# Attention of four experts on Trainium2: one written-out pipeline over 256 heads, with the row maxima split on GpSimd

## The chip, the cores and the metric

One core of a Trainium2 chip runs the whole kernel in one launch. The metric is the device time of an execution in microseconds (us), the median of repeated runs. TensorE (PE) multiplies, VectorE (DVE) and ScalarE (ACT) work on its results, GpSimd (POOL) does small work between SBUF buffers, and SyncE's queue (SPq) issues the DMAs.

## The reference, cut to what matters

The kernel computes a small language-model tower. The change touches one part of it, the attention inside each of 4 experts, for 4 batches of 512 tokens (16 blocks), with 16 heads of 16 channels, followed by the input products of a two-way LSTM:

```python
q, k, v = (heads(q), heads(k), heads(v))
attn = softmax(einsum('bhqd,bhkd->bhqk', q, k) * SCALE)
o = einsum('bhqk,bhkd->bhqd', attn, v).transpose(0, 2, 1, 3).reshape(h.shape)
h = o @ aow + aob
zg = xt @ Wi + h @ Wh + b      # x @ Wi + b is made here for all steps and both ways; the recurrence adds h @ Wh
```

## The kernel before, in words

The stages run one after another: embedding, causal attention, router, `experts_encode`, `experts_attend`, `recurrence`, `experts_after`, a state-space layer and a mixer. `experts_attend` is what changes, with three lines of `recurrence` that read its result.

**A head.** q and k arrive as bfloat16 parts, 96 rows per head (`load_heads`, L864, twelve DMAs for half of a block's heads). `score` (L975, matmul L981) makes one of four 128x512 tiles of scores in bank 0 or 1, by turns; `largest` (L1049, L1051) takes the negated row maximum on VectorE and frees the bank. `split` (L1054 to L1068) makes three bfloat16 parts of the four maxima with four tiny, dependent VectorE instructions. `turn_maxima` (L984, L990) turns the parts into rows 96 to 98 of q with four small matmuls, and `keep_rows` (L1088, ScalarE) stores them. `score_t` (L994, L1003) makes a transposed tile of scores with the maximum already taken off, in banks 2 to 4, and `exponent` (L1091, L1096, ScalarE) makes the exponentials. `values` (L1006, L1014) multiplies four heads' exponentials by v side by side in bank 6, and `keep_values` (L1100) copies the result of four heads out.

**A block.** After its 16 heads a block's result is turned (`turn_values`, L909), divided by the softmax sums (`divide`, L917 and L919, VectorE), turned back (`turn_divided`, L927; `keep_divided`, L935), projected (`project`, L943; `keep_projected`, L950) and multiplied by the LSTM's input weights: 16 products of 128x512 with two matmuls each (`product`, L874, L883). `keep_product` (L888, L894, VectorE) adds a bias and writes into `zs`; `store_products` (L897) sends 2 MB per way to DRAM.

**Order.** `attend(e, b, products)` is one block of instructions on all engines, of 18 written-out steps. In step h stand the scores of head h, the turned maxima of head h-1 and the transposed scores of head h-2. The first block of an expert has `products=False`. The other three run in a loop and also carry the turning, projection and products of the block before: the turning at their start, one product in each step from 2 on. All these products use bank 7 alone (`BESIDE`), one matmul of a product between `score_t` 2 and `score` 2, the other behind `values`:

```python
if products and h >= 2:
    product(pe, h - 2, 0, BESIDE)     # before score(h, 2)
...
if products and h >= 2:
    product(pe, h - 2, 1, BESIDE)     # last of the step
```

A product's first matmul waits for `z_kept` of the product before (L883). On VectorE a step is `keep_product`, two `largest`, two `largest`, `split`. The products of an expert's last block stand in a block of their own, with nothing beside them and two banks (`ALONE`). At every boundary all engines meet and semaphores are cleared. `zs` is `[P, 2, S, BLOCKS]`, so a product's 512 values lie 32 bytes apart.

Of the kernel before, what the change touches and what calls it, by code (L numbers as in the profile page):

```python
# [820 lines left out]
RING = 8  # L821


def experts_attend(core, d):


# [11 lines left out]
    with ExitStack() as ctx:  # L838
# [4 lines left out]
        vx = core.sb(ctx, "bvx", [P, BT, NH, DH + 1])  # L843
# [11 lines left out]
        zs = core.sb(ctx, "bzs", [P, 2, S, BLOCKS])  # L855
        (loaded, filled, scored, maxed, part1, part2, part3, rested, rows_mm, rows_kept, scored_t, exped, valued, o_kept,
         o_turned, inverted, on_done, on_turned, oT_kept, a_mm, a_kept, z_mm, z_kept) = core.sems(
            "ba", "loaded filled scored maxed part1 part2 part3 rested rowsmm rowskept scoredt exped valued okept "
                  "oturned inverted on onturned oTkept amm akept zmm zkept")
        qk_in = core.sems("ba", "qkin0 qkin1")  # L860
        (vx_in,) = core.sems("ba", "vxin")
        z_stored = core.sems("ba", "zstored0 zstored1")

        def load_heads(sp, slab, half):  # L864
            heads = slice(half * NH // 2, (half + 1) * NH // 2)
            for side, dst in ((0, qp), (1, kp)):
                for n, pair in enumerate(PAIRS):
                    src = d["qk"][slab, side, pair[side]].rearrange("(h r) n -> r h n", r=DH)
                    sp.dma_start(dst[n * DH:(n + 1) * DH, heads], src[:, heads]).then_inc(qk_in[half], 16)

        BESIDE, ALONE = (7,), (7, 5)
        HEADS_IN = 2 * len(PAIRS) * 16

        def product(pe, n, k, banks):  # L874

            way, block = divmod(n, BLOCKS)
            if k == 0:
                if n == 0:
                    pe.wait_ge(a_kept, KH)
                elif n >= len(banks):  # L880
                    pe.wait_ge(z_kept, n - len(banks) + 1)
            at = ATT["wi"] + (way * KH + k) * G4 + block * P
            last = nc.tensor.matmul(bank[banks[n % len(banks)]][:], w[:, at:at + P], aT[:, k], start=k == 0,  # L883
                                    stop=k == KH - 1)
            if k == KH - 1:
                last.then_inc(z_mm, 1)

        def keep_product(dve, n, banks, e, b):  # L888

            way, block = divmod(n, BLOCKS)  # L890
            dve.wait_ge(z_mm, n + 1)
            if block == 0:
                dve.wait_ge(z_stored[way], 16 * (e * B + b) + 1)
            nc.vector.tensor_scalar(zs[:, way, :, block], bank[banks[n % len(banks)]][:],  # L894
                                    cols[:, COLS["lb"] + n:COLS["lb"] + n + 1], None, ALU.add).then_inc(z_kept, 1)

        def store_products(sp, way, e, b):  # L897

            sp.wait_ge(z_kept, BLOCKS * (way + 1))
            sp.dma_start(d["zx"][way, e, b], zs[:, way].rearrange("p t n -> p (t n)")).then_inc(z_stored[way], 16)  # L900

        turn_banks = [bank[2], bank[3], bank[4], bank[7]]
        project_banks = [bank[7], bank[4]]

        def turn_values(pe):

            for qt in range(BT):
                for g in range(4):
                    last = nc.tensor.transpose(turn_banks[qt][:, g * P:(g + 1) * P], o[:, g, qt * P:(qt + 1) * P],  # L909
                                               core.ident[:])  # L910
                last.then_inc(o_turned, 1)

        def divide(dve):
            for qt in range(BT):
                heads = turn_banks[qt][:].rearrange("p (h r) -> p h r", r=32)
                dve.wait_ge(o_turned, qt + 1)
                nc.vector.reciprocal(inv[:, qt], heads[:, :, DH]).then_inc(inverted, 1)  # L917
                dve.wait_ge(inverted, qt + 1)
                nc.vector.tensor_tensor(on[:, qt], heads[:, :, 0:DH],  # L919
                                        inv[:, qt].unsqueeze(2).broadcast_to([P, NH, DH]), ALU.mult).then_inc(on_done, 1)  # L920

        def turn_divided(pe):

            for qt in range(BT):
                pe.wait_ge(on_done, max(qt + 1, 2))
                for k in range(KH):
                    last = nc.tensor.transpose(turn_banks[k][:, qt * P:(qt + 1) * P],  # L927
                                               on[:, qt, k * NH // KH:(k + 1) * NH // KH].rearrange("p h r -> p (h r)"),
                                               core.ident[:])
            last.then_inc(on_turned, 1)  # L930

        def keep_divided(act):
            act.wait_ge(on_turned, 1)
            for k in range(KH):
                nc.scalar.activation(oT[:, k], turn_banks[k][:], ACT.Copy).then_inc(oT_kept, 1)  # L935

        def project(pe):

            pe.wait_ge(oT_kept, KH)
            for m in range(KH):  # L940
                for k in range(KH):
                    at = ATT["aow"] + k * DM + m * P
                    last = nc.tensor.matmul(project_banks[m][:], w[:, at:at + P], oT[:, k], start=k == 0,  # L943
                                            stop=k == KH - 1)
                last.then_inc(a_mm, 1)

        def keep_projected(act):
            for m in range(KH):
                act.wait_ge(a_mm, m + 1)
                nc.scalar.activation(aT[:, m], project_banks[m][:], ACT.Identity,  # L950
                                     bias=cols[:, COLS["aob"] + m:COLS["aob"] + m + 1]).then_inc(a_kept, 1)

        def attend(e, b, products):


            with nc.Block() as block:
                @block.sync
                def _(sp):
                    if not products:
                        sp.dma_start(w[:], d["w_attend"][e]).then_inc(loaded, 16)  # L960
                        sp.dma_start(cols[:], d["cols"][e]).then_inc(loaded, 16)
                    load_heads(sp, e * B + b, 1)
                    sp.dma_start(vx[:].rearrange("p t h r -> p (t h r)"), d["vx"][e * B + b]).then_inc(vx_in, 16)
                    sp.wait_ge(scored_t, BT * NH // 2)
                    load_heads(sp, e * B + b + 1, 0)
                    if products:
                        for way in range(2):
                            store_products(sp, way, e, b - 1)
                    sp.wait_ge(qk_in[0], HEADS_IN)
                    if not products:  # L970
                        sp.wait_ge(loaded, 32)

                @block.tensor
                def _(pe):
                    def score(h, qt):  # L975

                        if h == NH // 2 and qt == 0:
                            pe.wait_ge(qk_in[1], HEADS_IN)
                        if BT * h + qt >= 2:
                            pe.wait_ge(maxed, BT * h + qt - 1)  # L980
                        nc.tensor.matmul(bank[qt % 2][:], qp[0:KROWS, h, qt * P:(qt + 1) * P], kp[0:KROWS, h],  # L981
                                         start=True, stop=True).then_inc(scored, 1)

                    def turn_maxima(h):  # L984

                        pe.wait_ge(part3, h + 1)
                        if h > 0:
                            pe.wait_ge(rows_kept, h)
                        for qt in range(BT):
                            last = nc.tensor.matmul(bank[5][KROWS:KROWS + 3, qt * P:(qt + 1) * P],  # L990
                                                    maxparts[:, h % 2, qt], ident16[:], start=True, stop=True)
                        last.then_inc(rows_mm, 1)

                    def score_t(h, kt):  # L994

                        n = BT * h + kt
                        if kt == 0:
                            pe.wait_ge(rows_kept, h + 1)
                        if products and n == 2:
                            pe.wait_ge(a_kept, KH)  # L1000
                        if n >= 3:
                            pe.wait_ge(exped, n - 2)
                        nc.tensor.matmul(bank[2 + n % 3][:], kp[:, h, kt * P:(kt + 1) * P], qp[:, h], start=True,  # L1003
                                         stop=True).then_inc(scored_t, 1)

# [171 lines left out]
        with nc.Fori(0, E - 1) as e:  # L1177
            expert(e, False)
# [826 lines left out]
```

## Time and profile before

| | us |
|---|---|
| median of 3 runs | 5915.8 (5911.99 to 5916.03) |
| the profiled execution | 5917.21, its span 5915.4 |
| `experts_attend` within the span | 779 to 2475 |
| `recurrence` | about 2475 to 5353 |
| mean granted TensorE clock | 0.963 of full speed |

The profile lists for each engine what it did and what it waited for. An instruction is named by line, engine and operation, then output<-input. A product or any other float32 matmul leaves two MATMUL records. "xN" in the timeline merges N instructions: the time beside it is from the first's start to the last's end.

### The profile page before, as it was taken

The page shows a single profiled execution, that of the slowest core. Times are in us where ns is not written, and L with a number is a line of the kernel's source. Part 1 is how long each engine was busy: PE and PEld are TensorE (multiplying, and loading weights), DVE is VectorE, ACT ScalarE, POOL GpSimd, SP SyncE. Part 2 cuts the span into 40 slices and gives each one's busy share as a digit, 9 for nine tenths or more (in the row PEclk, how much of TensorE's full clock was granted, in tenths as well). Part 3 has the DMA queues.
Part 4 walks back from the last instruction along what each step waited for, and adds up shares of the span by engine and source line. Part 5 has one row for each costly group of instructions (what it writes and reads, how often), then busy time and mean ns, then how long its engine had stood idle before and what let it go on. Part 6 is the DMA issues. An engine that isn't in the chain of part 4 may idle for free. (4 is left out here: it accounts for less than half of the span.)

```text
span 5915.4 us, 261478 instructions
## 1 busy us (share of the span) xinstructions
PE 5379.3 (91%) x108704; PEld 3590.6 (61%) x108704; DVE 4411.6 (75%) x20301; ACT 2334.2 (39%) x8423; POOL 944.5 (16%) x4109
## 2 busy tenths in 40 slices
PE   7878879989889998699999999999999999998895
PEld 4545523323323333288888888888888888884442
DVE  4546567666676676699999999999999999993224
ACT  2334444444354354433333333333333333333332
POOL 0000000000000000033333333333333333330000
PEclk9989989989989999899999999999999999999997
DMA  0003353334343334401111011111011111002110
GB/s 12 0 20 119 112 105 79 73 82 86 86 78 84 93 58 82 153 15 36 26 31 36 20 30 36 28 29 36 21 29 36 23 34 36 16 19 79 58 43 11
DMA packets 378664, 302.83 MB, mean 51 GB/s; under 512 B 146074, under 2 KB 358682, under 8 KB 373563
## 3 DMA queue, kind: packets, MB, share of 16 engines
q1 hardware_dynamic: 378510, 301.15, 21.4%
q8 instruction: 52, 0.85, 0.1%
q14 instruction: 102, 0.83, 0.0%
HBM read 182.09 MB, written 120.59 MB: 51 GB/s over the span
## 5 line engine op out<-in xcount | busy, mean ns | idle before, releaser
L1318 PE MATMUL bank<-lparts,lstate 128*32 128x256 bf16 x98304 | 2784.8, 273 | 103.2 <-DVE lstate L1364 55.5
L1318 PEld LDWEIGHTS bank<-lparts,lstate 128*32 128x32 bf16 x98304 | 2459.1, 97 | 429.4 <-DVE lstate L1364 252.4
L1395 ACT ACTIVATE ltc<-lgc 128x16 f32<-128x16 f32 x2049 | 442.6, 216 | 1763.8 <-DVE lgc L1350 1763.5
L1329 DVE STREAM_TRANSPOSE ltz<-bank 128x256 f32<-128x256 f32 x2048 | 920.8, 450 | 98.3 <-PE bank L1318 19.9
L1051 DVE TENSOR_REDUCE bnegmax<-bank 128x1 f32<-128x512 f32 x1024 | 650.1, 679 | 257.0 <-PE bank L981 255.7
L1411 POOL TENSOR_TENSOR wh<-lgate,ltc 128x16 f32<-128x16 f32 x2052 | 465.6, 227 | 1936.7 <-ACT ltc L1395 1862.5
L1096 ACT ACTIVATE wh<-bank 128x512 f32<-128x512 f32 x1024 | 554.9, 598 | 296.9 <-PE bank L1003 290.0
L1418 POOL COPY ltz<-wh 128x64 f32<-128x64 f32 x2048 | 605.8, 296 | 0.0
L883 PE MATMUL bank<-xT,bw 128*128 128x512 f32 x1024 | 537.0, 626 | 56.6 <-DVE bzs L894 50.2
L1336 DVE TENSOR_TENSOR lhalf<-ltz 128x128 f32<-128x128 f32 x2048 | 576.8, 282 | 12.1 <-POOL ltz L1418 11.4
L1346 DVE TENSOR_TENSOR lprod<-lgate,lgc 128x32 f32<-128x32 f32 x2049 | 472.7, 231 | 46.2 <-ACT lgc L1391 46.2
L1390 ACT ACTIVATE lgate<-lz 128x48 f32<-128x48 f32 x2048 | 499.8, 244 | 0.4
L894 DVE TENSOR_SCALAR bzs<-bank,bcols 128x512 f32<-128x512 f32 x256 | 292.3, 1142 | 251.9 <-PE bank L883 251.4
L981 PE MATMUL bank<-bkp,bqp 96*128 96x512 bf16 x1024 | 346.8, 410 | 121.5 <-DVE bnegmax L1051 37.6
L1340 DVE TENSOR_TENSOR lz<-lhalf 128x64 f32<-128x64 f32 x2048 | 438.6, 214 | 0.0
L1391 ACT ACTIVATE lgc<-lz 128x16 f32<-128x16 f32 x2048 | 408.2, 199 | 0.0
L1285 POOL MEMSET lstate<- 128x512 f32 x1 | 0.5, 525 | 2474.6 <-POOLq L61 2474.6
L981 PEld LDWEIGHTS bank<-bkp,bqp 96*128 96x128 bf16 x1024 | 98.0, 100 | 454.4 <-DVE bnegmax L1051 264.9
L883 PEld LDWEIGHTS bank<-xT,bw 128*128 128x128 f32 x1024 | 168.0, 189 | 332.4 <-DVE bzs L894 162.5
L1354 DVE TENSOR_TENSOR lstate<-lgate,ltc 128x16 f32<-128x16 f32 x2050 | 366.9, 179 | 3.3 <-ACT ltc L1395 0.3
L1359 DVE TENSOR_TENSOR lstate<-lstate 128x16 f32<-128x16 f32 x2048 | 347.8, 170 | 0.0
L1364 DVE TENSOR_TENSOR lstate<-lstate 128x16 f32<-128x16 f32 x2048 | 338.5, 165 | 0.0
(211 smaller groups left out, 4848.0 us busy)
## 6 DMA issues: line engine op xcount, KB each, us to landing
zx<-bzs SPq DMA_DIRECT2D x32, 2048.0 KB, 6.8
wh<-zx SPq DMA_DIRECT2D x64, 1024.0 KB, 7.4
bqp<-qk SPq DMA_DIRECT2D x198, 128.0 KB, 4.7
bkp<-qk SPq DMA_DIRECT2D x198, 128.0 KB, 7.9
qk<-eparts SPq DMA_DIRECT2D x96, 256.0 KB, 2.6
hs<-wh SPq DMA_DIRECT2D x32, 512.0 KB, 5.8
cmemT<-hs SPq DMA_DIRECT2D x32, 512.0 KB, 4.3
bw<-in_w_attend SPq DMA_DIRECT2D x4, 2304.0 KB, 11.5
```

The source lines that it names most:

```text
L883: last = nc.tensor.matmul(bank[banks[n % len(banks)]][:], w[:, at:at + P], aT[:, k], start=k == 0, stop=k == KH - 1)
L981: nc.tensor.matmul(bank[qt % 2][:], qp[0:KROWS, h, qt * P:(qt + 1) * P], kp[0:KROWS, h], start=True, stop=True).then_inc(scored, 1)
L1051: nc.vector.tensor_reduce(negmax[:, h, qt:qt + 1], bank[qt % 2][:], AX.X, ALU.max, negate=True).then_inc(maxed, 1)
L1096: nc.scalar.activation(pT[:, h % RING, kt], bank[2 + n % 3][:], ACT.Exp).then_inc(exped, 1)
L1318: last = nc.tensor.matmul(bank[x][32 * q:32 * q + 32, 0:256], top[:, x, e, k].rearrange("p m r -> p (m r)"), parts[:, way, g, k, n, e, q], ...
L1329: nc.vector.transpose(tz[:, x].rearrange("p (n w) -> p n w", w=SLOT)[:, :, 0:32], bank[x][:, 0:256].rearrange("p (n c) -> p n c", n=BLOCKS ...
L1336: nc.vector.tensor_tensor(half[:, x], rows[:, 1:3], rows[:, 3:5], ALU.add).then_inc(paired[x], 1)
L1346: nc.vector.tensor_tensor(prod[:, x], gate[:, x, 0:2], gc[:, x], ALU.mult).then_inc(multiplied[x], 1)
L1390: nc.scalar.activation(gate[:, x], z[:, x, 0:3], ACT.Sigmoid)
L1395: nc.scalar.activation(tc[:, x], gc[:, x, 1], ACT.Tanh).then_inc(tanhed[x], 1)
L1411: return nc.gpsimd.tensor_tensor(out.rearrange("p k (e b) -> p k e b", e=2), units(gate[:, x, 2]), units(tc[:, x]), ALU.mult)
L1418: nc.gpsimd.tensor_copy(rows, zx[:, way, i // ZX_STEPS % 2, 8 * g:8 * g + 8, at].rearrange("p r n -> p n r")).then_inc(placed[x], 1)
```

## The change

Both kinds of block, the loops over blocks and experts and the lone products go. One block of instructions is written out for 256 heads (step j is head j) and ends with the last block's turning and products. The turning of a block now stands in steps 6 to 10 after its last head's step, its 16 products in the eleven steps behind those, as 1, 2, 1, 2, ... products a step, all through bank 7; both matmuls of a product stand together. `turn_maxima` moves behind the products. The tail alone uses banks 7, 5, 0 and 1. GpSimd does `split`. Weights are loaded in three pieces, each as its last use is over, and v has two buffers. `zs` becomes `[P, 2, S/16, BLOCKS, 16]`: 16 values of a product stand side by side, and `recurrence` reads that order. The copy of block 0's q and k behind the last block's in DRAM goes. The other helpers (`score_t`, `values`, `exponent` and so on) do the same work with running counts.

```diff
+ZX_STEPS = 16
...
-        vx = core.sb(ctx, "bvx", [P, BT, NH, DH + 1])
+        vx = core.sb(ctx, "bvx", [P, 2, BT, NH, DH + 1])
...
-        zs = core.sb(ctx, "bzs", [P, 2, S, BLOCKS])
...
+        zs = core.sb(ctx, "bzs", [P, 2, S // ZX_STEPS, BLOCKS, ZX_STEPS])
...
+        TURN_AT, PRODUCTS_AT = 6, 11
+        PRODUCTS_IN_STEP = (1, 2, 1, 2, 1, 2, 1, 2, 1, 2, 1)
+        LAST_STEP = HEADS + 6
+        LATE_BANKS = (7, 5, 0, 1)
+        def products_of(j):
+            at = (j - PRODUCTS_AT) % NH
+            slab = (j - PRODUCTS_AT) // NH - 1
+            if slab < 0 or at >= len(PRODUCTS_IN_STEP):
+                return slab, 0, 0
+            first = sum(PRODUCTS_IN_STEP[:at])
+            return slab, first, first + PRODUCTS_IN_STEP[at]
+        def turned_in(j):
+            slab = (j - TURN_AT) // NH - 1
+            return (slab, (j - TURN_AT) % NH) if 0 <= slab < SLABS - 1 else (slab, -1)
...
+        def product_bank(slab, n):
+            return bank[LATE_BANKS[n % len(LATE_BANKS)] if slab == SLABS - 1 else 7]
+        def turn_bank(slab, n):
+            return bank[(2, 3, 4, 7)[n] if slab == SLABS - 1 else 7]
...
+                    if 0 < slab < SLABS:
+                        sp.wait_ge(scored_t, BT * NH * slab)
+                        load_heads(slab, 1)
+                    if slab >= 2:
+                        store_products(slab - 2, 1)
+                        if (slab - 2) % B == B - 1 and slab < SLABS:
+                            sp.wait_ge(z_mm, NH * (slab - 1))
+                            load_in_weights((slab - 1) // B, 1)
+                            load_columns((slab - 1) // B)
+                    if slab < SLABS - 1:
+                        if slab > 0:
+                            sp.wait_ge(valued, NH * slab)
+                        load_values(slab + 1)
+                        sp.wait_ge(scored_t, BT * NH * slab + BT * NH // 2)
+                        load_heads(slab + 1, 0)
+                    if slab > 0:
+                        if slab == SLABS:
+                            sp.wait_ge(valued, NH * SLABS)
+                            sp.dma_start(core.wh[:], d["wh"]).then_inc(wh_in, 16)
+                        if slab % B == 0 and slab < SLABS:
+                            sp.wait_ge(a_mm, KH * slab)
+                            load_out_weights(slab // B)
+                        store_products(slab - 1, 0)
...
+                for j in range(LAST_STEP):
+                    slab, at = turned_in(j)
+                    made, first, end = products_of(j)
+                    if j < HEADS:
+                        score(j, 0)
+                        score(j, 1)
+                    if 2 <= j < HEADS + 2:
+                        for kt in range(3):
+                            score_t(j - 2, kt)
+                    if at == 1:
+                        turn_values(slab, 1)
+                    elif at == 2:
+                        turn_values(slab, 3)
+                    elif at == 3:
+                        turn_divided(slab, 0)
+                    elif at == 4:
+                        project(slab, 0)
+                    elif end > first:
+                        for k in range(KH):
+                            product(made, first, k)
+                    if j < HEADS:
+                        score(j, 2)
+                        score(j, 3)
+                    if 2 <= j < HEADS + 2:
+                        score_t(j - 2, 3)
+                    if at == 0:
+                        turn_values(slab, 0)
+                    elif at == 1:
+                        turn_values(slab, 2)
+                    elif at == 3:
+                        turn_divided(slab, 1)
+                    elif at == 4:
+                        project(slab, 1)
+                    elif end > first + 1:
+                        for k in range(KH):
+                            product(made, end - 1, k)
+                    if 1 <= j < HEADS + 1:
+                        turn_maxima(j - 1)
...
+                def keep_product(slab, n):
...
+                        dve.wait_ge(z_stored[way], 16 * slab)
+                    nc.vector.tensor_scalar(zs[:, way, :, block],
+                                            product_bank(slab, n)[:].rearrange("p (c t) -> p c t", t=ZX_STEPS),
+                                            cols[:, COLS["lb"] + n:COLS["lb"] + n + 1], None, ALU.add).then_inc(z_kept, 1)
...
+                for j in range(LAST_STEP + 1):
+                    slab, at = turned_in(j)
+                    earlier, first_before, end_before = products_of(j - 1)
+                    made, first, end = products_of(j)
+                    if end_before > first_before + 1:
+                        keep_product(earlier, end_before - 1)
+                    if at == 1:
+                        divide(slab, 0)
+                    elif at == 2:
+                        divide(slab, 2)
+                    if j < HEADS:
+                        largest(j, 0)
+                        largest(j, 1)
+                    if end > first:
+                        keep_product(made, first)
+                    if at == 1:
+                        divide(slab, 1)
+                    elif at == 2:
+                        divide(slab, 3)
+                    if j < HEADS:
+                        largest(j, 2)
+                        largest(j, 3)
...
+            @block.gpsimd
+            def _(pool):
+                def split(j):
+                    negated = negmax[:, j % NH]
+                    parts = [maxparts[:, j % 2, :, n] for n in range(3)]
+                    pool.wait_ge(maxed, BT * (j + 1))
+                    if j >= 2:
+                        pool.wait_ge(rows_mm, j - 1)
+                    nc.gpsimd.tensor_copy(parts[0], negated).then_inc(part1, 1)
+                    pool.wait_ge(part1, j + 1)
+                    if j > 0:
+                        pool.wait_ge(part3, j)
+                    nc.gpsimd.tensor_tensor(rest[:], negated, parts[0], ALU.subtract).then_inc(rested, 1)
+                    pool.wait_ge(rested, j + 1)
+                    nc.gpsimd.tensor_copy(parts[1], rest[:]).then_inc(part2, 1)
+                    pool.wait_ge(part2, j + 1)
+                    nc.gpsimd.tensor_tensor(parts[2], rest[:], parts[1], ALU.subtract).then_inc(part3, 1)
+                for j in range(HEADS):
+                    split(j)
...
+                def keep_divided(slab, k):
+                    act.wait_ge(on_turned, KH * slab + k + 1)
+                    if k == 0 and slab > 0:
+                        act.wait_ge(a_mm, KH * slab)
+                    nc.scalar.activation(oT[:, k], turn_bank(slab, k)[:], ACT.Copy).then_inc(oT_kept, 1)
...
-            "p (w f g t n) -> p w f g t n", w=2, f=2, g=E * B, t=ZX_STEPS)
+            "p (w f g n t) -> p w f g n t", w=2, f=2, g=E * B, t=ZX_STEPS)
...
-            sp.dma_start(zx[:, way, buf].rearrange("p g t n -> p g (t n)"),
+            sp.dma_start(zx[:, way, buf].rearrange("p g n t -> p g (n t)"),
...
-                    nc.gpsimd.tensor_copy(rows, zx[:, way, i // ZX_STEPS % 2, 8 * g:8 * g + 8, at].rearrange(
+                    nc.gpsimd.tensor_copy(rows, zx[:, way, i // ZX_STEPS % 2, 8 * g:8 * g + 8, :, at].rearrange(
```

ScalarE's step is `keep_values` (every fourth), `keep_divided(1)` or `keep_projected(1)` where due, three `exponent`, `keep_divided(0)` or `keep_projected(0)` where due, the fourth `exponent`, `keep_rows`.

## Rows read from the trace of the kernel before

**Rows 1.** The profile's page: the span, and the busy time of each engine.
```profile
span 5915.4 us, 261478 instructions
PE 5379.3 (91%) x108704; PEld 3590.6 (61%) x108704; DVE 4411.6 (75%) x20301; ACT 2334.2 (39%) x8423; POOL 944.5 (16%) x4109
```
**Rows 2.** Windows: window, length, busy us (x instructions) per engine, PEclk, DMA share, GB/s.
```profile
779.00:2475.00 1696.00, 1515.92 (x6656) 532.62 (x6656) 1123.67 (x2432) 786.70 (x1411) 0.00 (x0) 0.95 0.39 86
...
782.30:852.70 70.40, 62.68 (x322) 17.42 (x323) 50.42 (x128) 47.22 (x85) 0.00 (x0) 0.90 0.48 88
853.00:953.50 100.50, 91.39 (x415) 32.05 (x412) 69.58 (x152) 48.99 (x88) 0.00 (x0) 0.98 0.37 74
...
1154.67:1203.51 48.84, 36.15 (x96) 17.70 (x97) 21.02 (x24) 3.74 (x5) 0.00 (x0) 0.89 0.31 120
```
**Rows 3.** Timeline, one head with a product: start us, us, instruction, idle before and releaser.
```profile
895.20 1.26 DVE L1051 TENSOR_REDUCE bnegmax<-bank 128x1 f32<-128x512 f32 x2
...
895.41 1.13 PE L883 MATMUL bank<-xT,bw 128*128 128x512 f32 x2
...
896.38 0.60 PE L981 MATMUL bank<-bkp,bqp 96*128 96x512 bf16 x2
...
896.80 1.29 DVE L1051 TENSOR_REDUCE bnegmax<-bank 128x1 f32<-128x512 f32 x2 [0.34 <-PE bank L981]
...
896.90 0.38 PE L990 MATMUL bank<-bident,bmaxparts 128*3 128x128 bf16 x4
...
897.54 1.05 PE L1014 MATMUL bank<-wh,bvx 128*17 128x512 f32 x8
...
898.12 0.18 DVE L1060 CAST bmaxparts<-bnegmax 128x4 bf16<-128x4 f32 x1
...
898.52 1.13 PE L883 MATMUL bank<-xT,bw 128*128 128x512 f32 x2
...
899.49 0.60 PE L981 MATMUL bank<-bkp,bqp 96*128 96x512 bf16 x2
...
899.69 1.14 DVE L894 TENSOR_SCALAR bzs<-bank,bcols 128x512 f32<-128x512 f32 x1 [0.78 <-PE bank L883]
...
899.92 0.81 PE L1003 MATMUL bank<-bqp,bkp 99*128 99x512 bf16 x3
900.34 1.57 ACT L1096 ACTIVATE wh<-bank 128x512 f32<-128x512 f32 x3 [1.80 <-PE bank L1003]
...
900.89 1.12 PE L883 MATMUL bank<-xT,bw 128*128 128x512 f32 x2 [0.15 <-DVE bzs L894]
```
**Rows 4.** Timeline, one head of a block without products.
```profile
818.40 0.61 PE L981 MATMUL bank<-bkp,bqp 96*128 96x512 bf16 x2
...
822.12 0.61 PE L981 MATMUL bank<-bkp,bqp 96*128 96x512 bf16 x2
```
**Rows 5.** Timeline, the start of a block that turns and projects the block before.
```profile
953.57 1.03 PE L981 MATMUL bank<-bkp,bqp 96*128 96x512 bf16 x2 [2.41 <-PEq L61]
...
954.40 3.07 PE L909 MATMUL bank<-ident,bo 128*128 128x128 f32 x16
...
955.49 0.26 DVE L917 RECIPROCAL binv<-bank 128x16 f32<-128x16 f32 x1
955.79 0.42 DVE L919 TENSOR_TENSOR xn<-bank,binv 128x256 f32<-128x256 f32 x1
```
**Rows 6.** Lines, shapes kept apart: two VectorE operations; busy us, mean ns, idle before.
```profile
L894 DVE TENSOR_SCALAR bzs<-bank,bcols 128x512 f32<-128x512 f32 x256 | 292.3, 1142 | 251.9 <-PE bank L883 251.4
...
L740 DVE TENSOR_SCALAR eqk<-bank,ecols 128x512 f32<-128x512 f32 x32 | 24.0, 751 | 61.0 <-PE bank L660 61.0
```
**Rows 7.** Lines, shapes kept apart: a small GpSimd operation of the recurrence.
```profile
L1411 POOL TENSOR_TENSOR wh<-lgate,ltc 128x16 f32<-128x16 f32 x2052 | 465.6, 227 | 1936.7 <-ACT ltc L1395 1862.5 <-issue 37.3 <-POOLq L1261 36.8
```
**Rows 8.** Timeline, the end of the stage.
```profile
2437.67 27.73 PE L883 MATMUL bank<-xT,bw 128*128 128x512 f32 x64 [0.78 <-ACT xT L950]
...
2475.03 0.53 POOL L1285 MEMSET lstate<- 128x512 f32 x1 [2474.58 <-POOLq L61]
```

More of the change, by code:

```diff
@@ L862, in experts_attend @@
         z_stored = core.sems("ba", "zstored0 zstored1")
[L864 to L871, printed above, removed]
@@ L872, in experts_attend @@
-        HEADS_IN = 2 * len(PAIRS) * 16
[L874 to L951, printed above, removed]
@@ L1122, in experts_attend, with project_bank @@
+        def turned_in(j):
[5 more added lines that the diff above has]
+            return bank[(2, 3, 4, 7)[n] if slab == SLABS - 1 else 7]
+        def project_bank(slab, n):
+            return bank[(4, 7)[n] if slab == SLABS - 1 else 7]
         with nc.Block() as block:
@@ L1124, in _, with load_heads @@
             def _(sp):
-                sp.dma_start(d["qk"][E * B], d["qk"][0]).then_inc(filled, 16)
-                load_heads(sp, 0, 0)
-                sp.wait_ge(qk_in[0], HEADS_IN)
-                sp.wait_ge(filled, 16)
+                def load_heads(slab, half):
+                    heads = slice(half * NH // 2, (half + 1) * NH // 2)
+                    for side, dst in ((0, qp), (1, kp)):
+                        for n, pair in enumerate(PAIRS):
+                            src = d["qk"][slab, side, pair[side]].rearrange("(h r) n -> r h n", r=DH)
+                            sp.dma_start(dst[n * DH:(n + 1) * DH, heads], src[:, heads]).then_inc(qk_in[half], 16)
@@ new lines, in load_values, with load_out_weights, load_in_weights @@
+                def load_values(slab):
+                    sp.dma_start(vx[:, slab % 2].rearrange("p t h r -> p (t h r)"), d["vx"][slab]
+                                 ).then_inc(vx_in[slab % 2], 16)
+                def load_out_weights(e):
+                    sp.dma_start(w[:, 0:ATT["wi"]], d["w_attend"][e, :, 0:ATT["wi"]]).then_inc(out_w_in, 16)
+                def load_in_weights(e, way):
+                    lo, hi = (ATT["wi"] + (way + n) * KH * G4 for n in range(2))
+                    sp.dma_start(w[:, lo:hi], d["w_attend"][e, :, lo:hi]).then_inc(wi_in[way], 16)
@@ new lines, in _ @@
+                load_out_weights(0)
+                load_columns(0)
+                for way in range(2):
+                    load_in_weights(0, way)
+                for slab in range(SLABS + 1):
+                    if 0 < slab < SLABS:
[21 more added lines that the diff above has]
+                        store_products(slab - 1, 0)
+                        if slab % B == 0 and slab < SLABS:
+                            sp.wait_ge(z_mm, NH * (slab - 1) + BLOCKS)
+                            load_in_weights(slab // B, 0)
@@ L1177, in experts_attend, with largest, divide @@
-        with nc.Fori(0, E - 1) as e:
-            expert(e, False)
-        expert(E - 1, True)
+                def largest(j, qt):
+                    dve.wait_ge(scored, BT * j + qt + 1)
+                    if j >= NH and qt == 0:
+                        dve.wait_ge(part3, j - NH + 1)
+                    nc.vector.tensor_reduce(negmax[:, j % NH, qt:qt + 1], bank[qt % 2][:], AX.X, ALU.max,
+                                            negate=True).then_inc(maxed, 1)
+                def divide(slab, qt):
+                    heads = turn_bank(slab, qt)[:].rearrange("p (h r) -> p h r", r=32)
+                    dve.wait_ge(o_turned, BT * slab + qt + 1)
+                    if qt == 0 and slab > 0:
+                        dve.wait_ge(on_turned, KH * slab)
+                        dve.wait_ge(on_done, BT * slab)
+                    nc.vector.reciprocal(inv[:, qt], heads[:, :, DH]).then_inc(inverted, 1)
+                    dve.wait_ge(inverted, BT * slab + qt + 1)
+                    nc.vector.tensor_tensor(on[:, qt], heads[:, :, 0:DH],
+                                            inv[:, qt].unsqueeze(2).broadcast_to([P, NH, DH]), ALU.mult).then_inc(on_done, 1)
```

373 lines of the change are left out of this document (179 added, 194 removed).

## The prediction

> **What bounds the kernel now.** I read the page first. PE is busy for 91% of the span [rows 1], but that is an average over stages, so the stage that changes is read alone: 1696 us long, PE 1516, VectorE 1124, ScalarE 787 busy [rows 2]. PE is the fullest engine, and its records overlap, so 1516 is no measure of what it must do. The windows by block show three kinds of time: a first block of an expert 70.4 us, a block with products about 100.5, the lone products 48.8 [rows 2]. Four times (70.4 + 3 x 100.6 + 48.8) is 1684, the stage within 1%.
>
> Then the timeline of one head with a product, which lasts 5.48 us (895.41 to 900.89) [rows 3]. Its chain closes on itself: the first matmul of a product until 896.38; scores, turned maxima and values until 898.52; the second matmul; 0.20 after its end, at 899.69, VectorE's copy; it ends at 900.83 and frees bank 7; the next product starts 0.06 later. The copy is a link of this chain. VectorE's splitting (898.12 to 898.91) is not: the copy behind it still waits 0.78 for PE [rows 3].
>
> A head without products takes 3.72 us [rows 4]. There the chain is score 0, maxima 0 and 1, score 3, a transposed score, turned maxima, values. By the durations below it gives 3.74, again without the splitting. So 256 x 0.8 = 205 us of splitting leave VectorE, and by these chains none of it is time of the stage. What is to be had lies in the single-bank chain, in the boundaries (2.41 us of idle PE, then turning with little beside it [rows 5]) and in four lone tails.
>
> **Durations for the walk**, from rows 3 where no other group is named. A score or a transposed score issues in 0.215 (two from 899.49 to 899.92); its reader starts 0.42 after it (896.38 to 896.80). A maximum: 0.58 apart, 0.68 long; a score that waits for it starts 0.14 after its end (VectorE ends at 896.46; the PE pair ends at 896.98, so its second began at 896.60). Turned maxima 0.41 and values 1.08, each with a weight load that nothing hides (their starts at 896.90, 897.54 and 898.52, with one transposed score of 0.215 between them). Exponentials 0.49 apart. A product with both matmuls together: 27.73/16 = 1.73 [rows 8], and 0.09 for its exposed load, 1.82. Four transposes 16 records in 3.07, so 0.77, with the load 0.86 [rows 5]. A division 0.72 (955.49 to 956.21) [rows 5].
>
> **The copy of a product.** Before, its writes lie 32 bytes apart and 512 values take 1142 ns. The nearest row with the same operation, PSUM source and side-by-side writes takes 751 [rows 6]. After, 16 values lie side by side. Bounds: 751 and 1142. I take 751, as it shares all but the pattern that the change removes. The Trainium skill (SBUF — State Buffer, section on door 1, the DMA port swizzle) says that accesses need two hits on each 16-byte line for full bandwidth, which speaks for write lines as the cause. Against it, VectorE: DVE Perf Modes (section on the TRN2 errata) prices PSUM to SBUF at 120 + 512 cycles, 658 ns, with no word of strides; by that rule the layout buys nothing. No row tells the two apart.
>
> **New steps, walked with score 0 at time 0.** All have scores 0, 1 and three transposed scores until 1.07.
> - One product: product 1.07 to 2.90; scores 2, 3 and a transposed score to 3.55; turned maxima 3.95; values 5.03. VectorE copies from 3.10, reduces from 3.69 and 4.27, done 4.95; the next score 1 (5.25) needs 5.09. Step **5.03**. With a slow copy (0.97 to the next instruction) the last maximum ends at 5.33, and score 1 waits 0.23: 5.26.
> - Two products: the second shares bank 7, so it waits for the copy (3.10 + 0.75 + 0.06 = 3.91, not 3.55), ends 5.73; values end **7.22**. Slow copy: 7.61.
> - Turning: step 6 is the 3.74 and four transposes, **4.58**. Step 7 has eight; its third turn waits for a division behind the second (1.93 + 0.20 + 0.72 = 2.85): **5.26**. Step 8: **4.06**. Step 9: the second turn back waits for ScalarE, which copies the first only behind three exponentials (ends 2.94): **5.35**. Step 10: two projections of 1.82, the second behind a ScalarE copy of 0.69: **7.16**. Sum 26.4.
>
> A block of 16 steps: 26.4 + 6 x 5.03 + 5 x 7.22 = 92.7, against 100.6, or 106 as the mean of an expert with its first block and tail.
>
> **The sum.** The stage starts about 3 us earlier (one boundary of [rows 5] and the wait for a DRAM copy; between 0 and 5): first score 779.3 instead of 782.3. 22 steps without products: 16 x 3.72 and six without values at about 3.5, half clock at the start included (the first block's 70.4 less its other steps leaves 22 for six), 81. Steps 22 to 261: 15 x 92.7 = 1390, less 9, as the last six have no scores and are paced by bank 7. Tail 48.8 less the shorter last copy and a boundary's idle time, 48. The end: 779.3 + 81 + 1381 + 48 = 2289, against 2475.0 [rows 8]: **-186**. The profiled execution took 5917.2, its span 5915.4, the median is 5915.8, so the new median is 5915.8 - 186 = 5730. The walk's durations are those at full granted clock; before, the windows with boundaries show 0.98 and the tail 0.89 [rows 2], and an unbroken stream gives no cause to fall below.
>
> **What I cost at nothing, and its cover.** GpSimd's splitting: four dependent instructions on four values. Its nearest row is 227 ns for 16 values [rows 7]; bounds 0.16 (VectorE's) and 0.4 each with the waits, 0.7 to 1.6 a head; I take 1.0. A head's maxima are done at 2.92 of a step without products, and the turned maxima that need them stand at 3.74 + 2.25 = 5.99: 3.0 of cover, 3.6 in a step with one product. Without cover each us would cost 240. Moved turned maxima: `keep_rows` ends about 0.65 behind them, the transposed score that needs it comes 1.5 behind. DMAs on SyncE's queue: a block's second half of heads is issued at step 2 and needed at step 8, some 35 us later; the first half 7 steps ahead; the stores of one way have 10 steps until `zs` is written again. The tightest is an expert's bias columns: behind the last products of the expert before, a 2 MB store and 1 MB of weights, needed 22 us later at the projection. If they are late, ScalarE's `keep_projected` stands, behind it an exponential, and PE; three times at most 10 us. Recurrence: GpSimd's read keeps its inner stride of 512 bytes, and it has 1937 us idle there [rows 7]; 0, between -2 and +5.
>
> **The rivals.** (a) *The copy stays at 1142.* For it: the page's formula above, and that no row shows the new pattern; against it: 751. Each block is 6 x 0.23 + 5 x 0.39 = 3.3 longer, x15 = 50: 5780. Chance 0.13. (b) *Loads late at each expert, or instruction supply of the written-out code adds some 0.15 us a step.* For it: the waits above; against it: 18 steps run before with no such gap. Some 35 us: 5765. Chance 0.09. (c) *Waits overlap better than walked.* PE alone needs 24.6 + 6 x 5.03 + 5 x 6.85 = 89.1 a block, 54 us less: 5676. Chance 0.05. (d) *Slower: GpSimd's splitting outruns its cover.* The turned maxima wait on `part3`, and the values and next scores queue behind them. It decides from 3.6 + 186/240 = 4.4 us a head on, 1.1 per instruction; at 5 us it costs 240 x 1.4 = 336, so 5915.8 + 150 = 6066. Against it: 227 ns [rows 7]. Chance 0.03. (e) *VectorE was the bound after all*, so its 205 us come off too: 5525. The 0.78 of waiting [rows 3] excludes most of it. 0.01.
>
> **How the numbers follow.** The forecast keeps 0.69, with 30 us to either side for the walk's errors and the start. 5700 to 5788 takes in (a) and (b) and leaves out (c), (d), (e) and some of the tail. About 0.2%, 12 us, is what a measurement of this kernel can tell from no change: every case but (d) is faster by more; 0.02 for unforeseen sums near zero.
>
> **What would show it.** The profile after should have steps of 5.0 and 7.2 us by turns, a block period near 93, L894's operation near 750 ns, bank-7 waits of 0.4 in the two-product steps, GpSimd at about 1 us a head, no PE wait on it, and a stage end near 2289. It is wrong if the copy still takes 1142, if PE waits for `bmaxparts`, if the period is above 97, or if the recurrence changes length by over 5 us.

## The result, and the profile after

The kernel after takes 5641.0 us (median of 4 runs, 5639.3 to 5643.7) against 5913.9 us of the kernel before (4 runs made beside them), a ratio of 0.9539 with a 95% interval of 0.9523 to 0.9556. It is faster by 273 us. I had said 5730, with 5700 to 5788 as the range: the sign and the chain of waits held, the size did not, and the prices of two groups of matmuls in my sum are why.

The page of the profile after, its span and busy times (PE, VectorE and GpSimd answer to [rows 1]), and two of its costliest groups:

```profile
span 5639.1 us, 260566 instructions
...
PE 5230.6 (93%) x108704; PEld 3565.2 (63%) x108704; DVE 4163.9 (74%) x19277; ACT 2326.0 (41%) x8421; POOL 1144.1 (20%) x5133
...
L1052 PE MATMUL bank<-xT,bw 128*128 128x512 f32 x1024 | 487.3, 600 | 17.0 <-DVE bzs L1135 16.2
...
L1135 DVE TENSOR_SCALAR bzs<-bank,bcols 128x512 f32<-128x512 f32 x256 | 192.3, 751 | 317.8 <-PE bank L1052 317.8
```

L1135 is the copy of a product. It takes 751 ns, to the nanosecond what I took from L740 [rows 6]. The products still wait for it (16.2 us of PE), because they all use the single bank 7.

The windows of the kernel after, with the columns of rows 2: the stage, its first 22 steps, one period of 16 steps, and the tail:

```profile
779.00:2204.00 1425.00, 1368.26 (x6656) 514.04 (x6656) 873.53 (x1410) 778.26 (x1409) 202.08 (x1024) 0.99 0.47 101
785.28:862.10 76.82, 72.22 (x380) 20.64 (x380) 55.27 (x88) 58.18 (x105) 16.95 (x86) 0.88 0.63 103
2031.12:2117.96 86.84, 84.73 (x417) 32.15 (x416) 54.54 (x89) 48.56 (x89) 12.63 (x64) 1.00 0.28 67
2157.87:2204.10 46.23, 34.49 (x96) 16.10 (x96) 14.46 (x24) 2.46 (x4) 0.00 (x0) 0.95 0.76 316
```

The stage ends at 2204.1 instead of 2475.0. Read against rows 2, a block (the period, from a step to the same step of the next block) costs 86.84 us at full granted clock instead of 100.5 at 0.98. VectorE's busy time in the stage fell from 1124 to 874, ScalarE's stayed (787 and 778). My working compared with this, part by part: first score 785.3 instead of 779.3 (+6); 22 steps 76.8 instead of 81 (-4); steps 22 to the end 1295 instead of 1381 (-86); tail 47 instead of 48 (-1); what follows the stage 5.4 us shorter instead of 0 (-5). The sum is -90, and all of it that matters is the block: 86.8 where I had 92.7.

One step with one product and one with two, from PE's timeline of the kernel after; [rows 3] is the step of before:

```profile
2101.36 0.60 PE L972 MATMUL bank<-bkp,bqp 96*128 96x512 bf16 x2
...
2104.60 0.38 PE L990 MATMUL bank<-bqp,bkp 99*128 99x512 bf16 x1
2104.91 0.22 PE L980 MATMUL bank<-bident,bmaxparts 128*3 128x128 bf16 x1
2104.92 0.62 PE L1002 MATMUL bank<-wh,bvx 128*17 128x512 f32 x3
2104.96 0.33 PE L980 MATMUL bank<-bident,bmaxparts 128*3 128x128 bf16 x3
2105.13 1.02 PE L1002 MATMUL bank<-wh,bvx 128*17 128x512 f32 x5
2106.09 0.67 PE L972 MATMUL bank<-bkp,bqp 96*128 96x512 bf16 x2
...
2109.97 1.98 PE L1052 MATMUL bank<-xT,bw 128*128 128x512 f32 x4 [0.19 <-DVE bzs L1135]
...
2113.06 0.60 PE L972 MATMUL bank<-bkp,bqp 96*128 96x512 bf16 x2
```

The first step is 4.73 us long (I had 5.03), the second 6.97 (7.22). The new thing is in the middle. The records of the turned maxima (L980) and of the values (L1002) interleave: the first of values starts 0.01 us after the first turned maximum. From the first turned maximum to the next score pass 1.18 us. I had added 0.41 and 1.08, 1.49, from a kernel in which a transposed score always stood between them.

The turning steps, from the same view:

```profile
2077.78 0.67 PE L972 MATMUL bank<-bkp,bqp 96*128 96x512 bf16 x2
...
2081.71 0.60 PE L972 MATMUL bank<-bkp,bqp 96*128 96x512 bf16 x2
...
2082.80 0.60 PE L1014 MATMUL bank<-ident,bo 128*128 128x128 f32 x4
2083.24 0.63 PE L972 MATMUL bank<-bkp,bqp 96*128 96x512 bf16 x2
...
2085.97 0.60 PE L972 MATMUL bank<-bkp,bqp 96*128 96x512 bf16 x2
...
2089.46 0.60 PE L972 MATMUL bank<-bkp,bqp 96*128 96x512 bf16 x2
...
2092.53 0.63 PE L1023 MATMUL bank<-ident,xn 128*128 128x128 f32 x4 [0.69 <-ACT xT L1214]
...
2094.26 0.60 PE L972 MATMUL bank<-bkp,bqp 96*128 96x512 bf16 x2
...
2101.36 0.60 PE L972 MATMUL bank<-bkp,bqp 96*128 96x512 bf16 x2
```

The five steps are 3.93, 4.26, 3.49, 4.80 and 7.10 us long, together 23.6 (I had 4.58, 5.26, 4.06, 5.35 and 7.16, together 26.4).

Four transposes issue in 0.44 us (2082.80 to 2083.24), not in the 0.86 I took from [rows 5]. That row stood in a stretch of low granted clock. The kernel before shows it itself. The window of that place comes first, then another block of the same trace, whose 16 transposes take 1.75 us up to the next score, 0.44 for four:

```profile
953.57:957.40 3.83, 3.83 (x19) 3.35 (x20) 2.94 (x8) 0.00 (x0) 0.00 (x0) 0.58 0.96 229
```

```profile
852.42:854.60 2.18, 2.18 (x19) 1.97 (x20) 1.73 (x4) 0.00 (x0) 0.00 (x0) 1.00 0.49 113
```

```profile
852.85 1.91 PE L909 MATMUL bank<-ident,bo 128*128 128x128 f32 x16
854.60 0.60 PE L981 MATMUL bank<-bkp,bqp 96*128 96x512 bf16 x2
```

A mean of 0.58 says that most of the stretch was at the lower of the two clock levels, 1.2 GHz. It follows the boundary at which PE stood idle for 2.41 us [rows 5]; the other block followed 2.22 us of idle time and was at 1.00, so such a gap did not always bring the lower level. In the kernel after the transposes stand in an unbroken stream, and its period shows 1.00.

### The profile page after: what moved, and what is told of

The parts are those of the page before. It is cut to its first block and busy times, and to the rows that moved or that the text cites. A ratio compares the mean times of both kernels' runs of the same rounds, so it can differ in the third digit from the quotient of the medians.

```text
span 5639.1 us, 260566 instructions
## 1 busy us (share of the span) xinstructions
PE 5230.6 (93%) x108704; PEld 3565.2 (63%) x108704; DVE 4163.9 (74%) x19277; ACT 2326.0 (41%) x8421; POOL 1144.1 (20%) x5133
## 5 line engine op out<-in xcount | busy, mean ns | idle before, releaser
L1052 PE MATMUL bank<-xT,bw 128*128 128x512 f32 x1024 | 487.3, 600 | 17.0 <-DVE bzs L1135 16.2
L1177 POOL CAST bmaxparts<-bnegmax 128x4 bf16<-128x4 f32 x256 | 49.4, 193 | 1870.4 <-DVE bnegmax L1114 1870.4
L1135 DVE TENSOR_SCALAR bzs<-bank,bcols 128x512 f32<-128x512 f32 x256 | 192.3, 751 | 317.8 <-PE bank L1052 317.8
L972 PE MATMUL bank<-bkp,bqp 96*128 96x512 bf16 x1024 | 325.9, 388 | 34.2 <-DMA bkp<-qk 27.1
L1418 DVE TENSOR_TENSOR lgc<-lprod 128x16 f32<-128x16 f32 x2049 | 339.3, 166 | 0.0
```

The source lines that it names most:

```text
L1052: last = nc.tensor.matmul(product_bank(slab, n)[:], w[:, at:at + P], aT[:, k], start=k == 0, stop=k == KH - 1)
```

## The experiments

**Undoing one part: the place of the turned maxima.**

```diff
+                    if 1 <= j < HEADS + 1:
+                        turn_maxima(j - 1)
                     if 2 <= j < HEADS + 2:
                         score_t(j - 2, 3)
...
-                    if 1 <= j < HEADS + 1:
-                        turn_maxima(j - 1)
                     if j >= 6:
                         values((j - 6) // 4, (j - 6) % 4)
```

> The kernel after, with the turned maxima moved back ahead of the fourth transposed score, so that they no longer stand beside the values. Theory (the four small matmuls of the turned maxima run partly at the same time as the first matmuls of values when nothing stands between them, which took the pair from 1.49 to 1.17 us): 0.25 to 0.30 us more in each of 256 heads, 64 to 77 us, so 5705 to 5718 us. Rival (the missing 89 us are all in the turning steps, whose transposes I priced too high, and the place of the turned maxima is worth nothing): within 10 us of 5641.

Measured: 5649.7 us, 9 over the kernel after; as ratios to the kernel before 0.9556 (0.9539 to 0.9572) beside 0.9539 (0.9523 to 0.9556), whose intervals overlap. The expectation failed (64 to 77 more), and the rival's number came out. PE's timeline of this kernel says why the rival's reason is not right either:

```profile
2070.63 0.60 PE L972 MATMUL bank<-bkp,bqp 96*128 96x512 bf16 x2
...
2073.97 0.39 PE L980 MATMUL bank<-bident,bmaxparts 128*3 128x128 bf16 x4
2074.29 0.39 PE L990 MATMUL bank<-bqp,bkp 99*128 99x512 bf16 x1
2074.51 1.92 PE L1052 MATMUL bank<-xT,bw 128*128 128x512 f32 x4
...
2077.35 0.60 PE L972 MATMUL bank<-bkp,bqp 96*128 96x512 bf16 x2
...
2082.31 0.60 PE L972 MATMUL bank<-bkp,bqp 96*128 96x512 bf16 x2
```

A one-product step is 4.96 (+0.23), as the theory has it. A two-product step is 6.72 (-0.25): ahead of the second product the turned maxima do their work in time in which PE would wait for bank 7. The turning steps are level in sum (23.6). The period is 86.93, against 86.84. So in the blocks the place has two effects of one size that cancel. Outside them they do not: from the first score to the first projection the stage is 9.8 us longer here, since a step without products takes 3.71 instead of 3.49 and the granted clock rises later (0.58 instead of 0.92 in the 20 us that begin 15 us after the first score). The first score came 6.5 us earlier in this profile, which hides most of that.

**The same place in the kernel before.**

```diff
-                        if 1 <= h <= NH:
-                            turn_maxima(h - 1)
...
                         if h >= 2:
                             score_t(h - 2, 3)
+                        if 1 <= h <= NH:
+                            turn_maxima(h - 1)
                         if h >= 6:
                             values((h - 6) // 4, (h - 6) % 4)
```

> The kernel before, with only the turned maxima moved down to stand directly ahead of the values (and, on ScalarE, their copy behind the fourth exponential). Theory (side by side with values): the step with a product falls from 5.48 to about 5.18 and the one without from 3.72 to about 3.47, 65 to 77 us in all, so 5837 to 5849 us. Rival (the place is worth nothing): 5914, within 10 us.

Measured: 5897.7 us beside 5911.6, ratio 0.9975 (0.9965 to 0.9985), 14 us less: neither the 65 to 77 of the theory nor the rival's nothing. The steps with values do what was expected, 5.48 to 5.24 and 3.72 to 3.48. But PE's timeline at the start of a block shows what was overlooked, with the turned maxima now behind the projection (L943):

```profile
1067.05 3.70 PE L943 MATMUL bank<-xT,bw 128*128 128x512 f32 x8
1070.68 0.39 PE L990 MATMUL bank<-bident,bmaxparts 128*3 128x128 bf16 x4
...
1073.04 0.39 PE L1003 MATMUL bank<-bqp,bkp 99*128 99x512 bf16 x1 [0.69 <-ACT xT L950]
1073.27 1.02 PE L883 MATMUL bank<-xT,bw 128*128 128x512 f32 x2
```

From the start of the projection to the first product pass 6.22 us; in the kernel before it is 4.71 (1062.61 to 1067.32). The steps before a block's first values have nothing to stand beside and stay at 4.6. So the steps with values gain 0.24 each, one place loses 1.5, and from the start of a block to that of the next the mean of twelve fell only from 101.3 to 100.0 us.

**The place again, with the waits taken out.** First the second product, the second turn back and the second projection go behind the values:

```diff
-                    elif at == 3:
-                        turn_divided(slab, 1)
-                    elif at == 4:
-                        project(slab, 1)
-                    elif end > first + 1:
-                        for k in range(KH):
-                            product(made, end - 1, k)
...
                     if j >= 6:
                         values((j - 6) // 4, (j - 6) % 4)
+                    if at == 3:
+                        turn_divided(slab, 1)
+                    elif at == 4:
+                        project(slab, 1)
+                    elif end > first + 1:
+                        for k in range(KH):
+                            product(made, end - 1, k)
```

> The kernel after, with the second product of a two-product step, the second turn back and the second projection moved behind the turned maxima and the values. The waits for bank 7 and for ScalarE (0.27 us in a two-product step, about 0.5 and 0.35 us in the last two turning steps) then lie under 1.2 us of other TensorE work. If those waits are all that it changes: 15 x (5 x 0.27 + 0.85) = 33 us less, so about 5608 us. Rival (the wait only moves to the next step, where the next product or the scores stand behind VectorE): 5635 to 5650.

> The kernel a_second_last, with the turned maxima ahead of the fourth transposed score. In a_rows_apart the turned maxima cost 0.23 us more in one-product steps and gave 0.25 back in two-product steps, where they filled the wait for bank 7. With that wait gone from the step, the theory (turned maxima and values run side by side when adjacent, worth 0.23 to 0.25 us in every head) says about 0.24 x 250 = 60 us over a_second_last. Rival (what a_rows_apart showed, that the place is worth under 10 us in all, is general): within 10 us of a_second_last.

Measured: 5598.8 us (ratio 0.9467, 0.9451 to 0.9483) and 5649.0 (0.9554, 0.9538 to 0.9570). The first is 42 us under the kernel after, more than the 33 expected; its period is 83.98. A two-product step fell by 0.35 (6.97 to 6.62, expected 0.27) and the step of the second turn back by 0.82 (4.80 to 3.98, expected 0.5). It beats both kernels. The second is 50 us over the first, where I had said about 60. Here the place of the turned maxima is worth 0.23 us in a step with one product, 0.16 in a step with two and 0.6 in the five turning steps, 86.76 - 83.98 = 2.78 us in a block, 42 in fifteen. Some 10 more lie in the stage's first steps, part of them again a clock that rises later (0.58 instead of 0.93). The rival, that the place is worth nothing in general, is excluded. What waits ahead of PE's float32 products in the two kernels (waits of PE, 900 to 2100 us), first the kernel after, then a_second_last:

```profile
PE bank L1052 <- DVE bzs L1135: 13.3, 69, 0.2
PE bank L1023 <- ACT xT L1214: 9.6, 14, 0.7
PE bank L972 <- DVE bnegmax L1114: 2.9, 14, 0.2
```

```profile
PE bank L972 <- DVE bnegmax L1114: 2.9, 14, 0.2
PE bank L1052 <- DVE bzs L1135: 1.0, 2, 0.8
```

69 waits for the bank became 2, and ScalarE's 14 are gone.

**What runs side by side?** An attempt at the reason: the fourth matmul of values writes the same group of 32 rows as the turned maxima, the others do not.

```diff
-                    for c in range(4):
+                    for c in (3, 0, 1, 2):
```

> The kernel after, with the four matmuls of values issued in the order 3, 0, 1, 2 instead of 0, 1, 2, 3. The turned maxima come out on rows 96 to 98, the fourth matmul of values on rows 96 to 112, the others on rows 0 to 80. Theory (what runs side by side is work on different output rows): with the fourth first, values can't begin beside the turned maxima, the pair takes about 1.40 us again, and the time goes up as the step with one product does by 0.23 us, 256 x 0.23 = 59 us at most, less where a step waits anyway: 5680 to 5700 us. Rival (adjacency alone hides a weight load, whatever rows it writes): within 10 us of 5641.

Measured: 5639.1 us, ratio 0.9537 (0.9521 to 0.9553), no change. The timeline still interleaves, in another order:

```profile
2100.47 0.33 PE L980 MATMUL bank<-bident,bmaxparts 128*3 128x128 bf16 x3
...
2100.58 0.62 PE L1002 MATMUL bank<-wh,bvx 128*17 128x512 f32 x3
2100.63 0.22 PE L980 MATMUL bank<-bident,bmaxparts 128*3 128x128 bf16 x1
2100.69 1.02 PE L1002 MATMUL bank<-wh,bvx 128*17 128x512 f32 x5
...
2101.64 0.67 PE L972 MATMUL bank<-bkp,bqp 96*128 96x512 bf16 x2
```

1.17 us again from the first turned maximum to the next score. My theory that the first matmul of values must write other rows falls. That the two groups take 0.23 us less side by side than apart is shown (1.17 against 1.40); whether it is a hidden weight load, the narrow outputs or something else stays open.

**The layout of zs**, undone in the kernel after and alone in the kernel before:

```diff
-        zs = core.sb(ctx, "bzs", [P, 2, S // ZX_STEPS, BLOCKS, ZX_STEPS])
+        zs = core.sb(ctx, "bzs", [P, 2, S, BLOCKS])
```

> The kernel after, with the old order of the products in zs (values 32 bytes apart). If the write pattern sets the copy's 1142 ns, the copy takes 1142 again; by the measured steps a one-product step then waits 0.45 us more for its last maximum and a two-product step 0.39 for bank 7, 15 x (6 x 0.45 + 5 x 0.39) = 70 us, so 5711; by the prediction's own step lengths it would be 50, 5691. Rival (the copy is hidden and its length does not matter): 5641.

> The kernel before, with only the new order of zs. The copy is a link of the closed chain of a step with a product there (first matmul, scores, turned maxima, values, second matmul, copy), so its 0.39 us come off in each of 192 such steps: 75 us, 5837 us, more than the 51 us that the same layout is worth in the kernel after. Rival (a maximum or ScalarE ends last as soon as the copy is shorter): 5870 to 5914.

Measured: 5692.3 us (ratio 0.9626, 0.9610 to 0.9643), 51 over the kernel after, and 5840.6 us beside 5912.4 (ratio 0.9882, 0.9865 to 0.9898), 72 less. The copy in the first, then in the second:

```profile
L1135 DVE TENSOR_SCALAR bzs<-bank,bcols 128x512 f32<-128x512 f32 x256 | 293.9, 1148 | 338.3 <-PE bank L1052 338.3
```

```profile
L894 DVE TENSOR_SCALAR bzs<-bank,bcols 128x512 f32<-128x512 f32 x256 | 191.9, 750 | 278.9 <-PE bank L883 278.4
```

So the write pattern is the cause of 1142 ns, and the same 0.39 us is worth more in the kernel before (72 us, 75 expected), where the copy is a link of the closed chain, than in the pipeline, where about half of it is covered. In a_old_layout the period is 90.28, 3.44 over the kernel after. The 5711 that I expected from the measured steps was too much; the prediction's 3.3 a block was nearer. The two-product step waits 0.39 longer for bank 7, and score 1 behind it waits for a maximum, 0.31, five times each. My 3.3 had six waits of 0.23 in the one-product steps, so its terms agree only in their sum. PE's timeline has both waits:

```profile
2000.81 1.98 PE L1052 MATMUL bank<-xT,bw 128*128 128x512 f32 x4 [0.58 <-DVE bzs L1135]
...
2009.22 0.39 PE L972 MATMUL bank<-bkp,bqp 96*128 96x512 bf16 x1 [0.20 <-DVE bnegmax L1114]
```

**The splitting back on VectorE.**

```diff
                     if j < HEADS:
                         largest(j, 2)
                         largest(j, 3)
+                        split(j)
```

The four instructions of `split` are issued by VectorE here and GpSimd has none.

> The kernel after, with the splitting of the maxima back on VectorE at the end of each of its steps. Theory (the splitting is on no chain that sets the stage): 0 us in the steps with products and without, at most 0.5 us in two or three turning steps where a division stands behind it, so 5641 to 5666 us. Rival (VectorE's relief is a large part of the gain; 256 x 0.8 us of splitting come back): over 5740 us.

Measured: 5651.7 us (ratio 0.9554, 0.9537 to 0.9571), 11 over the kernel after by the medians, inside what the theory allowed; the two intervals overlap. The period is 87.65, 0.82 more, and steady from block to block, so 12 us are seen in the trace too. All of it lies in two turning steps (4.45 for 3.93 and 3.78 for 3.49), where PE waits for a maximum; the steps with products are unchanged. That VectorE's 205 us of splitting were time of the stage is excluded.

**The pipeline alone**, with layout, splitting and place of the turned maxima all undone, so the three edits above in one kernel:

```diff
-        zs = core.sb(ctx, "bzs", [P, 2, S // ZX_STEPS, BLOCKS, ZX_STEPS])
+        zs = core.sb(ctx, "bzs", [P, 2, S, BLOCKS])
...
+                    if 1 <= j < HEADS + 1:
+                        turn_maxima(j - 1)
                     if 2 <= j < HEADS + 2:
                         score_t(j - 2, 3)
...
                         largest(j, 3)
+                        split(j)
```

> The kernel after with three of its parts undone at once: old order of zs, splitting on VectorE, turned maxima ahead of the fourth transposed score. What is left is the written-out pipeline. If the parts add up: 5641 + 51 + 11 + 9 = 5712 us, so the pipeline alone is worth some 200 of the 273 us. If they cover for each other (a slow copy makes room for the splitting and for the turned maxima): nearer 5692. If together they make VectorE the bound (its step is then 4 x 0.6 + 0.8 + 1.5 x 1.0 = 4.7 us with products): over 5740.

Measured: 5704.8 us, ratio 0.9647 (0.9631 to 0.9663), period 90.5. The parts nearly add up (5712 by the sum). In the periods they cover each other by 0.7 us a block (86.84 + 3.44 + 0.82 + 0.09 = 91.2). The written-out pipeline is worth about 208 of the 273 us, the layout some 50, splitting and place some 10 each, counted by undoing each alone.

## Why the prediction was wrong

- **The chains.** Right. The stage is set by PE and its waits on bank 7, not by VectorE; the splitting, which fills 205 us of VectorE, is worth 11.
- **The copy at 751 ns.** Right, and rival (a)'s 50 us is what a_old_layout measured (51). The Trainium skill (SBUF — State Buffer, section on door 1) wants two hits on each 16-byte line for full bandwidth, and the runs agree: 1142 to 1148 ns with values 32 bytes apart, 750 to 751 side by side. By the formula of the Trainium skill (VectorE: DVE Perf Modes, section on the TRN2 errata), 658 ns as an estimate for either pattern, the layout would have changed nothing, and the runs decide against that.
- **GpSimd's splitting, 1.0 us a head, covered.** Right. It takes 1.0 (2099.10 to 2100.11), four instructions 0.27 apart, and no gap of PE's matmuls is put down to it. The profile does put a gap of the weight loads (PEld) down to it, at the end of the last turning step:

```profile
2093.57 0.21 POOL L1185 TENSOR_TENSOR bmaxparts<-brest,bmaxparts 128x4 bf16<-128x4 f32 x1
...
2098.26 1.98 PE L1037 MATMUL bank<-xT,bw 128*128 128x512 f32 x4
...
2099.10 0.19 POOL L1177 CAST bmaxparts<-bnegmax 128x4 bf16<-128x4 f32 x1 [5.32 <-DVE bnegmax L1114]
...
2099.91 0.20 POOL L1185 TENSOR_TENSOR bmaxparts<-brest,bmaxparts 128x4 bf16<-128x4 f32 x1
2100.18 0.09 PEld L980 LDWEIGHTS bank<-bident,bmaxparts 128*3 128x3 bf16 x2 [0.76 <-POOL bmaxparts L1185]
```

  But the turned maxima at 2100.18 are those of the head before (`turn_maxima(j - 1)`), whose splitting ended at 2093.78. They start 1.92 us after the second projection began, just as they start 1.92 us after a product began (2109.97 to 2111.89), so it is the projection that they stand behind. The splitting that ended at 2100.11 is used at 2104.91.
- **The step that failed: "A block of 16 steps: 26.4 + 6 x 5.03 + 5 x 7.22 = 92.7."** Measured 23.6 + 6 x 4.73 + 5 x 6.97 = 86.8. Two terms were mis-sized. The first is the pair "turned maxima 0.41 and values 1.08", 1.49. Even apart it takes 1.40 (1.62 from 896.90 to 898.52 in [rows 3], less the 0.215 of the transposed score; the same in a_rows_apart), so 0.09 was misread; side by side it takes 1.18. The walk only added durations and put the overlap of neighbouring groups at nothing. That is 0.31 in each of 16 steps, 5.0 a block. The second is "four transposes 0.86", a price from a stretch at a granted clock of 0.58. At 1.00 a group issues in 0.44 ahead of a score and in 0.53 to 0.59 ahead of turned maxima. The five turning steps gain some 1.7 by it, since one of the six groups lies under a wait for ScalarE. I had written that the durations were those at full clock; for rows 5 that was not so, and the same trace had the price at full clock. Smaller terms, some for and some against, take 0.8 back (the three matmuls ahead of the pair take 0.75, not 0.65, a first product 1.71, not 1.83, and both projections start later than I had). The net is 5.9 us in each of 15 blocks, 88 us, which is the whole miss. In the 22 steps without products the pair side by side made 3.49 of 3.72, 4 us in all.
- **Rival (c), waits that overlap better.** It gave 5676 with "PE alone needs 89.1 a block". The kernel after is under that floor, because the floor was built from the same two prices. No rival questioned the prices themselves.
- **The start.** 785.3, not 779.3: SyncE's first load of heads was issued at 770.2, and its data were waited for. Opposite in sign and small. The profiles of the eight kernels with the pipeline, which do the same up to there, have the first score anywhere from 778.8 to 785.3, so one profile can't settle a term of 3 us. The loads elsewhere (rival b) are not seen in the period, which repeats within 0.01 us.

## What to carry to other kernels

A duration is a price at the granted clock of its own window: look at that window, and where it shows less than 1.00, look for the same work elsewhere in the trace. Durations add only in the order in which they were measured; where a change makes two small groups of matmuls neighbours, their sum needs a bound from below as well. A releaser that the profile names is inferred: ask the code which instruction is really waited for. And what comes last in a single-buffered step is worth choosing: in a_second_last work put into the wait for a bank cost nothing, and one reorder after the fact was worth another 42 us.

## What the runs showed that I had not expected

Four matmuls with 3 output rows and four with 17 take 1.17 us next to each other and 1.40 us with a full-width matmul between them, whichever of the four comes first. An order of instructions can gain 0.23 us in one kind of step and lose 0.25 in another, so that undoing it alone shows next to nothing (9 us), while it is worth 50 us once the wait is gone. The recurrence ran 2835.6 us from its first to its last matmul after the change and 2840.2 before. That is not shown to be the new layout: a_second_last, with the same recurrence as the kernel after, took 2839.1, and a_old_layout, with the old order, 2838.0.
